# A mixture-of-experts transformer block on one core: planes added by TensorE at the end, and expert maps computed by quarters of the partitions

## The reference, cut to what matters

```
scores = softmax(xf @ gate_w.T);  idx = top_k(scores + gate_b, 2)
w = scores at idx
h  = silu((x @ w1[e] + b1[e]) * (x @ w3[e] + b3[e]))          # for the token's two experts e
y  = sum over its two experts of  w * (h @ w2[e] + b2[e])
z  = the same form with one shared expert (sw1, sw3, sw2), for every token
x  = x + (y + z)
```

## Time and profile before

| | |
|---|---|
| median of three runs | 709.68 us |
| the profiled execution, its time | 710.83 us |
| its span | 708.8 us, 20460 instructions |
| TensorE matmul busy | 655.8 us (93%) |
| VectorE busy | 537.3 us (76%) |
| ScalarE busy | 421.3 us (59%) |
| GpSimd busy | 508.7 us (72%) |
| mean granted TensorE clock | 0.96 of full |
| HBM | 33.76 MB read, 22.08 MB written |

### The profile page before, as it was taken

One profiled execution on the slowest core, in us unless ns is written; L12 is line 12 of the kernel. 1 busy time (PEld: TensorE's weight loads), 2 busy tenths in 40 slices (PEclk: granted clock), 3 DMA queues, 4 the chain that ended last, 5 costly groups with the idle time before them and its releaser, 6 DMA issues.

```text
span 708.8 us, 20460 instructions
## 1 busy us (share of the span) xinstructions
PE 655.8 (93%) x6788; PEld 551.9 (78%) x6788; DVE 537.3 (76%) x1513; ACT 421.3 (59%) x1166; POOL 508.7 (72%) x844
## 2 busy tenths in 40 slices
PE   8799999999988999999989999999898877999995
PEld 7477777777767999999976777777676667999994
DVE  5488999999854566655436879999998767778778
ACT  5367877776545333433434777777573764777773
POOL 5955488768765898886766676888777764777771
PEclk9899999999989999999997999999999987999998
DMA  5380000001422432334311110111030122333375
GB/s 175 106 334 24 6 29 28 29 29 36 158 75 84 131 101 65 97 100 114 92 38 31 31 32 17 48 44 59 20 90 32 34 72 63 99 97 101 96 252 187
DMA packets 45403, 57.67 MB, mean 81 GB/s; under 512 B 11379, under 2 KB 37142, under 8 KB 44630
## 3 DMA queue, kind: packets, MB, share of 16 engines
q1 hardware_dynamic: 36086, 38.11, 18.2%
q0 software_dynamic: 8640, 17.97, 7.4%
q10 hardware_dynamic: 576, 0.29, 0.2%
HBM read 33.76 MB, written 22.08 MB: 79 GB/s over the span
## 4 chain that ended last, share of the span: by engine, by line
PE 39%; DVE 24%; POOL 20%; issue 12%; ACT 2%; SPq 2%; DMA 1%; POOLq 0%; DVEq 0%; ACTq 0%
POOL results L1616 9%; PE S L2044 7%; PE ptp L2063 6%; DVE mx L1053 5%; DVE pr L1054 5%; PE M L1357 4%; PE S L1320 4%; POOL rows L612 4%; PE ptp L1340 3%; PE S L1322 3%; POOL xi L1609 3%; PE M L1408 2%; SPq L701 2%; PE S L2050 1%; PE ptp L1343 1%
## 5 line engine op out<-in xcount | busy, mean ns | idle before, releaser
L612 POOL DMA_INDIRECT rows<-out_rows,posi x128 | 127.8, 999 | 48.5 <-issue 28.5
L795 ACT ACTIVATE pT<-ptp 128x512 f32<-128x512 f32 (+1 forms) x192 | 94.2, 524 | 82.7 <-PE ptp L1340 75.5
L1053 DVE TENSOR_REDUCE mx<-S 128x16 f32<-128x1232 f32 x64 | 91.2, 1425 | 19.2 <-PE S L1322 18.6
L1616 POOL DMA_INDIRECT results<-early,xi x71 | 74.9, 1055 | 30.3 <-DVE early L1680 22.8
L1054 DVE TENSOR_TENSOR pr<-S,mx 128x1232 f32<-128x1232 f32 x64 | 92.2, 1441 | 2.2
L1914 POOL DMA_INDIRECT results<-early,xs x71 | 69.9, 984 | 33.2 <-issue 16.8
L1706 PE MATMUL S<-early,w1s 128*128 128x128 f32 x568 | 77.7, 280 | 4.8 <-DVE w1s L1673 3.3
L1716 PE MATMUL S<-first_w,early 128*128 x568 | 75.5, 276 | 0.7 <-DVE early L1680 0.7
L1706 PEld LDWEIGHTS S<-early,w1s 128*128 128x128 f32 x568 | 70.4, 195 | 7.4 <-issue 6.1
L1357 PE MATMUL M<-pT,vm 128*32 128x128 f32 (+1 forms) x2048 | 70.2, 277 | 0.0
L1680 DVE TENSOR_SCALAR early<-S,xs 128x128 f32<-128x128 f32 x71 | 24.9, 351 | 59.8 <-PE S L1716 34.0
(11 more groups left out here) (220 smaller groups left out, 1556.3 us busy)
## 6 DMA issues: line engine op xcount, KB each, us to landing
xs<-rows SPq DMA_DIRECT2D x142, 66.0 KB, 1.9
first_w<-in_e_W SPq DMA_DIRECT2D x2, 2048.0 KB, 8.6
swap<-results SPq DMA_DIRECT2D x32, 128.0 KB, 2.2
first_w<-results SPq DMA_DIRECT2D x6, 512.0 KB, 8.6
rows<-out_rows,posi POOLq DMA_INDIRECT x128, 2.3
x_res<-in_x SPq DMA_DIRECT2D x1, 1536.0 KB, 8.1
W1r<-in_e_W SPq DMA_DIRECT2D x1, 1536.0 KB, 11.0
out_x<-x_res SPq DMA_DIRECT2D x3, 512.0 KB, 2.6
```

The source lines that it names most:

```text
L612: nc.gpsimd.indirect_dma_start(rows[:, :], bass.IndirectOffsetOnAxis(posi[:, k, n:n + 1], 0), out_rows[:, ring_slot(groups, n), k, :], Non ...
L795: nc.scalar.activation(pT[0:rows_of, G * r:G * r + count, :], ptp[q % 2][0:rows_of, 0:count, :], ACT.Exp, scale=SCALE)\
L1053: do(V.tensor_reduce(mx[:, :].rearrange("p (g j) -> p g j", g=G), sc, AX.X, ALU.max))
L1616: nc.gpsimd.indirect_dma_start(results[:, :], bass.IndirectOffsetOnAxis(xi[:, s:s + 1], 0), ys[:, s, :], None)\
```

## The change

It has two parts, which do not depend on each other.

**Maps by quarters.** A table of constants gets 14 more columns, which hold, on partition p, the numbers 14·(p // 32) to 14·(p // 32) + 13. The steps "tiles" and "maps" work on 14 columns in place of 55: each quarter of 32 partitions computes the map of its own 14 tiles. `mapped` says on which partition (0, 32, 64 or 96) and in which column the sequencers find tile i.

**The end.** VectorE adds the planes of the first 20 batches only (`HALVES` = 5 halves of four). For the last six shared units `narrow` is followed, for each batch, by a wait for the batch's piece and two more matmuls with the identity as weights and the two planes as moving data, which add into the same PSUM accumulation; VectorE's add of that PSUM into x then carries all of it. SP asks for the last piece of planes before it stores anything, and the stores of batches 16 to 31 wait for the adds of the shared results (`z_ready`).

```
+C_QUARTER = 716
+C_END = 730
+    c[:, C_QUARTER:C_END] = (p // 32)[:, None] * (C_END - C_QUARTER) + np.arange(C_END - C_QUARTER)[None, :]
...
-BETWEEN, HALVES_EARLY = (10, 18, 26), 7
+BETWEEN, HALVES = (10, 18, 26), 5
...
+def mapped(tiles, i, done):
+    row, at = (0, i) if i < done else ((i - done) // (C_END - C_QUARTER), done + (i - done) % (C_END - C_QUARTER))
+    return tiles[32 * row:32 * row + 1, at:at + 1]
...
-        count = SLOTS - done
+        count = C_END - C_QUARTER
...
-        slot = cst[:, C_SLOT:C_SLOT + count]
+        slot = cst[:, C_QUARTER:C_END]
...
-            steps.mark(V.tensor_scalar(st["emap"][:, done:SLOTS].bitcast(U32), ...))
+            steps.mark(V.tensor_scalar(st["emap"][:, done:done + count].bitcast(U32), st["slot_u"][:, 0:count], E - 1, None, ALU.bitwise_and))
...
-        V.tensor_copy(st["rowmap"][:, done:SLOTS], slot_row).then_inc(maps_done, 1)
+        V.tensor_copy(st["rowmap"][:, done:done + count], slot_row).then_inc(maps_done, 1)
...
-        ... eng.value_load(emap[0:1, n:n + 1]) ...      (and rowmap; in both feed-forwards)
+        ... eng.value_load(mapped(emap, n, EARLY)) ...
...
-ADDS_FROM = len(UNITS) + 2 - HALVES_EARLY - 2
+ADDS_FROM = len(UNITS) - 7
...
+    def with_planes(u):
+        return UNITS[u][0] == "shared" and UNITS[u][1] >= HALVES * HU
...
         def store(b0, b1):
-            sp.wait_ge(x_done, b1 // HU)
+            sp.wait_ge(x_done, min(b1 // HU, HALVES))
+            if b1 > HALVES * HU:
+                sp.wait_ge(z_ready, b1 // 2)
...
-            if c == len(PIECES) - 1:
-                for b0, b1 in STORES[:2]:
-                    store(b0, b1)
             load_results(c)
-        for b0, b1 in STORES[2:]:
+        for b0, b1 in STORES:
             store(b0, b1)
...
-            if u - 2 >= ADDS_FROM and halves < HALVES_EARLY:
+            if u - 2 >= ADDS_FROM and halves < HALVES:
                 add_results(halves)
...
-        for half in range(halves, B // HU):
+        for half in range(halves, HALVES):
             add_results(half)
...
                 for c in range(2):
-                                            start=(c == 0), stop=(c == 1))
+                                            start=(c == 0), stop=(c == 1 and not with_planes(u)))
+                if with_planes(u):
+                    b = UNITS[u][1] + at
+                    pe.wait_ge(results_in[piece_of(b)], landed[piece_of(b)])
+                    for k in range(2):
+                        last = nc.tensor.matmul(yp(u)[:, at, :], ident, yg[:, k, b, :], start=False, stop=(k == 1))
             last.then_inc(yp_ready, 1)
```

More of the change, by code:

```diff
@@ L50 @@
 C_BAND, C_COS, C_SIN, C_BEFORE, C_SLOT = 180, 260, 388, 516, 644
-C_END = 716
+C_QUARTER = 716
+C_END = 730
 ROOT = D ** 0.5
@@ L1261, in vector @@
         else:
-            steps.mark(V.tensor_copy(st["emap"][:, done:SLOTS], slot_e))
+            steps.mark(V.tensor_copy(st["emap"][:, done:done + count], slot_e))
         do(V.tensor_tensor(some_big, some_big, by_pair(step), ALU.mult))
         if nq > E:
-            steps.mark(V.tensor_scalar(st["emap"][:, done:SLOTS].bitcast(U32), st["slot_u"][:, 0:count], E - 1, None, ALU.bitwise_and))
+            steps.mark(V.tensor_scalar(st["emap"][:, done:done + count].bitcast(U32), st["slot_u"][:, 0:count], E - 1, None, ALU.bitwise_and))
         do(V.tensor_reduce(slot_row, some_big, AX.X, ALU.add))
@@ L1570, in expert @@
     def expert(eng, n):
-        return nc.s_assert_within(eng.value_load(emap[0:1, n:n + 1]), 0, E - 1,
+        return nc.s_assert_within(eng.value_load(mapped(emap, n, EARLY)), 0, E - 1,
                                   skip_runtime_bounds_check_because="VectorE bounds the map's entries by E - 1")
     def row_of(eng, i):
-        return nc.s_assert_within(eng.value_load(rowmap[0:1, i:i + 1]), 0, SHARED - 128,
+        return nc.s_assert_within(eng.value_load(mapped(rowmap, i, EARLY)), 0, SHARED - 128,
                                   skip_runtime_bounds_check_because="the map's rows are those of its experts' tiles")
@@ L1848, in expert, with piece_of @@
     def expert(eng, i):
-        return nc.s_assert_within(eng.value_load(emap[0:1, i:i + 1]), 0, E - 1,
+        return nc.s_assert_within(eng.value_load(mapped(emap, i, EARLY)), 0, E - 1,
                                   skip_runtime_bounds_check_because="VectorE bounds the map's entries by E - 1")
+    def with_planes(u):
+        return UNITS[u][0] == "shared" and UNITS[u][1] >= HALVES * HU
+    def piece_of(b):
+        return [c for c, (b0, b1) in enumerate(PIECES) if b0 <= b < b1][0]
     def row_of(eng, i):
-        return nc.s_assert_within(eng.value_load(rowmap[0:1, i:i + 1]), 0, SHARED - 128,
+        return nc.s_assert_within(eng.value_load(mapped(rowmap, i, EARLY)), 0, SHARED - 128,
                                   skip_runtime_bounds_check_because="the map's rows are those of its experts' tiles")
@@ L1996, in add_results @@
             b0 = half * HU
-            c = [c for c, (p0, p1) in enumerate(PIECES) if p0 <= b0 < p1][0]
+            c = piece_of(b0)
             dve.wait_ge(z_ready, (b0 + HU) // 2)
```

## The result

The changed kernel took 701.17 us in the median of four runs (700.11 to 706.61) beside 709.08 us for the kernel before (707.27 to 714.99, four runs): ratio 0.9892, 95% interval 0.9854 to 0.9929, that is 7.9 us less. The profiled execution has a span of 699.0 us, 9.8 less than before's 708.8.

The account below looks back on a forecast made before the run. VectorE was taken to bound layer 1's maps and the tail; maps -5.8 and tail +0.2 make -5.6 us, giving 705.2 for the profiled execution, 704.1 from the median, forecast as 704.0, range 702.0 to 707.2.

Parts of the forecast that it names:

- What bounds the kernel: VectorE's map operations hold TensorE in layer 1, not layer 0; in the tail VectorE still adds after TensorE stops.
- Maps: Layer 1's maps: shorter operations and the kept clock together save 5.8 us.
- The operations: Layer 1's maps: four large and five small VectorE operations on 14 columns instead of 55 save 4.11 us.
- The clock: Behind layer 1's maps: TensorE's clock does not fall after a shorter idle time, saving 1.7 us, bounds 0 to 1.80.
- rival (a): Layer 1's maps: the clock falls all the same, or GpSimd's later start is not made good; 705.8 us, chance 0.15.
- Rival (c): Layer 1's maps: some other wait holds TensorE, so the maps are not worth their length; 707.9 us, chance 0.08.
- GpSimd's later start: Routed units after layer 1's maps: GpSimd's sends start about 1.7 us worse against TensorE; cost 0, bound 0.5 us.
- The tail: End of the kernel: TensorE's added products and a new wait make it end at 706.5 against 706.28, +0.2 us.
- the wait for piece (16, 24): Tail, unit 46: TensorE waits 0.9 us for planes of batches 20 and 21, bounds 0 to 2.
- The rest of this term: Tail without the new wait: TensorE becomes the bound and ends at 705.6 against 706.28, a gain of 0.7 us.
- the chance of faster: Whole kernel: chance 0.24 of a time below 702.6 us, more than about 1% faster.
- rival (d): Tail, unit 46: TensorE waits for the first planes until the clock goes; 710.6 us, or 719.7 all low, chance 0.05.

Follow-up runs that it names:

- e1: Kernel before with only the maps' edit, in both layers, and the old end; ratio to before 0.9923, 5.5 us less.
- e3: e1 with layer 0 keeping its 55 map columns, so only layer 1 has the short maps; mean 705.2 us beside 705.1 for e1.
- e7_halves7: Changed kernel with `HALVES` = 7, TensorE adding planes of the last two units only; VectorE's last instruction ends 0.8 us later than with six halves.
- e8_warm_before: Kernel before with 13 unread products before each of two weight waits behind layer 1's maps; ratio 0.9967, maps' stretch 13.02 us instead of 14.64.
- e9_dose: Changed kernel with layer 1's compare issued five times instead of once; maps' stretch 12.38 us instead of 9.12, one execution.
- e4_whole: The changed kernel measured again unaltered, twelve runs; median 704.79 us, ratio to before 0.9928.
- e2_end_only: Changed kernel with the maps as before, so only the end is edited; tail 22.64 us against 22.69, ratio's interval holds 1 and 0.997.
- e12_whole_again: The changed kernel measured once more unaltered; ratio to before 0.9920.
- e5_old_order: Changed kernel with SP storing parts 0 and 1 before asking for the last planes; ratio to before 0.9986, tail 27.15 us.

## Why the prediction was wrong

**What bounds the kernel: right.** VectorE's map operations stood in TensorE's path in layer 1 and not in layer 0 (e1, e3), the routed units between them kept their pace (0.08 us of difference over 82 us), and the tail was VectorE's: with one of its eight halves moved to TensorE (e7_halves7) it is 1.2 us shorter.

**Maps: right, 5.5 us against 5.8.** The operations: 3.9 us against 4.1, from the rate of 1.034 ns a number, which held (0.49 us). The clock: 1.6 against 1.7 (e8_warm_before). That the gap of 1.3 us would not cost the clock held in every trace with the maps' edit but e9_dose, where the gap was made longer: TensorE waited 1.1 to 1.3 us at the first weight copy and 1.4 to 1.5 us at the second, the routed `widen`s took 1.58 us, and the stretch 9.05 to 9.22 us each time; rival (a) never came up. Rival (c) falls.

**GpSimd's later start: no cost**, as forecast; the distance from the third `widen` to the last routed one is the same in both kernels.

**The tail: the sum had +0.2, it is -0.6 to -0.1.** The term that was mis-sized is the wait for piece (16, 24), 0.9 us in the prediction. It is there in two of the six traces of this end, 0.25 to 0.28 us as the trace marks it and some 0.4 by the distance of the starts (e4_whole, e2_end_only), and absent in the other four (after, e12_whole_again, e9_dose, e5_old_order). The load's time itself was read rightly and was not the far end of six draws: the last of these loads took 10.2 to 11.8 us in every trace that has it. What scatters is the moment: in the eleven traces that show it, it landed 6.5 to 8.1 us behind the start of the last routed `widen`, and the first product with a plane wants it at 7.2. The kernel before has the 8.1, the latest of the eleven. The rest of this term, 0.7 us of gain with TensorE as the new bound at 3.08 us a unit, came out as 0.6 in after and e12.

```profile
685.42 0.71 PE L2084 MATMUL ptp<-first_w,cst 128*128 128x128 f32 x4 [0.25 <-DMA first_w<-results]
```

**The step that failed is the last one: the range.** The sum of 5.6 us was right: 5.7 by means over 28 and 79 runs. A little luck is in that, as the maps were taken 0.3 us too high and the tail 0.3 to 0.8 us too low; the terms as measured make 5.6 to 6.1 us, still inside the range, so no term of the sum explains a time of 701.17. The prediction noted that "the three runs before span 6 us", and used it for the chance of faster only (0.24 for a time below 702.6). The range was built from the bounds of the terms, as if what is measured were the kernel's mean. What is measured is the median of a few executions whose times scatter with a standard deviation of 2.65 us, and much of that goes with where the clock's low stretches fall; the median of four of them has a standard error of about 1.6 us, and the difference of two such medians 2.3. With two standard errors of the one, the range around 704.0 should have begun near 701, and then it holds 701.17. The same scatter is in the 9.8 us between the two profiled executions: 3.8 of them lie ahead of the change.

What I cannot show is why the first four runs lay low; that they were drawn from the same scatter is supported by the two repetitions and by the clock's correlation, not proved. Three of the first four lie at or below 701.55 us, and of the 24 later ones four do; of all ways to draw four out of the 28, 4% hold three or more of these seven. That is rare enough to keep another cause open. The later runs come from two chips that agree with each other; the record does not name the chip of the first four.

One slip in the chances changes nothing in the sum: rival (d) stands among "slower by over 1%", but its own first price, 710.6, is 0.1% above 709.68.

## What to carry to other kernels

Before a range is given, the scatter of the kernel's own runs belongs in it, next to the bounds of the terms; and when two profiled executions are compared, follow common points from the start and see how much of the difference lies ahead of the edit. A wait of TensorE of about 3 us can have two prices, its length and the clock behind it: the edit that shortened it from 3.25 to some 1.1 us earned both (3.9 and 1.6 us), and the one that lengthened it to 3.39 paid both (2.2 and 1.1). Moving adds from VectorE to TensorE pays only until TensorE is the bound; the best of the three splits tried was four units instead of six or two, and the end of the span showed it only after the stores behind it were spread.

## What the runs showed of the hardware that I had not expected

- Unread matmuls in TensorE's queue during a wait kept the granted clock at 1.00 through the whole maps' stretch, and it was 1.6 us shorter (e8_warm_before, one trace).
- The time of a run of one and the same kernel follows its mean granted clock, from 0.960 to 0.978 before: 10 us (after) and 12 us (before) between the fastest and the slowest execution, with 0.28 us of time (before) for each us at the lower level. Not every low stretch costs: at 24 us in the changed kernel's trace it cost nothing that can be seen, at 33 us in the trace before it fell on the first attention batches, and the lead of the other trace grew from 0.7 to 2.9 us there.
- The 512 KB loads of the planes, six of them issued within 3.2 us, landed 4.8, 6.0, 7.4, 10.8, 9.7 and 11.8 us after their issue (before); the last of them took 10.2 to 11.8 us in every trace that has it.
- Reading the maps from partitions 32, 64 and 96 by the sequencers costs nothing that the routed rhythm shows: it is 2.45 us a unit in both traces.
